# A graph attention and mixture-of-experts kernel: tiles in fill order, first weights loaded per tile, both expert results of a token side by side

## The reference

```
x = x + gnn(layernorm(x), edges, ...)          # two attention layers, 4 heads and 1 head
xf = layernorm(x)
probs = softmax(xf @ gate_w + gate_b);  top2_vals, top2_idx = top_k(probs, 2)
for each expert e:  h = gelu(xf @ W1[e] + b1[e]);  y = h @ W2[e] + b2[e]
out += (weight of e for the token, else 0) * y
x = x + out
```

## Time and profile before

| | us |
|---|---|
| median of 3 runs | 6120.17 |
| lowest, highest | 6066.71, 6154.52 |
| the profiled execution, its own time | 6092.53 |
| its span | 6090.7 |

### The profile page before, as it was taken

The page is one execution under the profiler, slowest core; times in us unless marked ns, Lnnn a source line. Parts: engine busy times, 40 slices in busy tenths (PEclk is TensorE's granted clock), DMA queues, the critical chain, the costliest instruction groups (busy, mean ns, idle before and its releaser), DMA issues. The chain is left out here.

```text
span 6090.7 us, 75071 instructions
## 1 busy us (share of the span) xinstructions
PE 3576.1 (59%) x12549; PEld 2299.2 (38%) x12550; DVE 3420.2 (56%) x8873; ACT 1636.8 (27%) x3595; POOL 3368.1 (55%) x3575
## 2 busy tenths in 40 slices
PE   5455555565555555554556666566666656624994
PEld 3233333333333333332333333333333333312773
DVE  7555555555555555555555555555555555531444
ACT  3222222222222222221233332322233333311222
POOL 4655555555555555555555555555655555644222
PEclk8666667766777777776676666666666676667997
DMA  4344444444444444443444444444444444442224
GB/s 127 104 109 108 105 108 110 109 107 106 109 108 109 110 110 110 110 104 86 111 114 114 115 114 114 113 114 114 114 113 114 114 113 114 118 137 86 91 64 155
DMA packets 321285, 670.43 MB, mean 110 GB/s; under 512 B 76855, under 2 KB 152773, under 8 KB 320938
## 3 DMA queue, kind: packets, MB, share of 16 engines
q0 software_dynamic: 170848, 469.37, 29.3%
q1 hardware_dynamic: 148585, 199.90, 11.5%
q10 hardware_dynamic: 1792, 0.53, 0.0%
HBM read 602.38 MB, written 75.12 MB: 111 GB/s over the span
## 5 line engine op out<-in xcount | busy, mean ns | idle before, releaser
L1002 POOL DMA_INDIRECT rows<-table,idx x3200 | 3031.4, 947 | 2086.8 <-issue 925.9
L1149 PE MATMUL bank<-rows,hit 128*128 128x260 f32 (+1 forms) x6464 | 2655.5, 553 | 2049.4 <-DVE acc L1257 1033.4
L1149 PEld LDWEIGHTS bank<-rows,hit 128*128 128x128 f32 x6464 | 1538.6, 265 | 2916.4 <-issue 1406.1
L1257 DVE TENSOR_TENSOR acc<-acc,bank 128x260 f32 (+1 forms) x3232 | 1356.4, 420 | 1385.5 <-remote 569.6
L1032 ACT ACTIVATE arg<-arg 128x32 f32<-128x32 f32 (+1 forms) x404 | 88.4, 219 | 3415.3 <-DVE arg L1237 2364.4
L1244 DVE TENSOR_TENSOR rows<-rows,bank 128x1024 f32<-128x1024 f32 x808 | 946.0, 1212 | 11.1 <-issue 9.7
L1211 DVE TENSOR_TENSOR hit<-bank,dst_loc 128x256 f32<-128x256 f32 x1616 | 671.7, 417 | 69.9 <-issue 58.6
L1222 DVE TENSOR_REDUCE bank<-bank 128x64 f32<-128x192 f32 (+1 forms) x404 | 115.4, 286 | 667.5 <-remote 598.8
L1026 ACT ACTIVATE hit_t<-gap,ones 128x1024 bf16<-128x1024 bf16 x404 | 463.8, 1148 | 20.3
L1021 ACT ACTIVATE gap<-loc,minus_node 128x1024 bf16<-128x1024 bf16 x404 | 462.6, 1145 | 11.7 <-DMA loc<-loc_row 11.5
L1138 PE MATMUL bank<-du,hit_t 128*128 x3232 | 340.9, 182 | 129.9 <-issue 127.6
(11 more groups left out here) (223 smaller groups left out, 2191.9 us busy)
## 6 DMA issues: line engine op xcount, KB each, us to landing
loc<-loc_row SPq DMA_DIRECT2D x404, 256.0 KB
rows<-table,idx POOLq DMA_INDIRECT x3200
sent<-zeros SPq DMA_DIRECT2D x202, 68.3 KB
xe<-sent SPq DMA_DIRECT2D x106, 128.5 KB
got<-back SPq DMA_DIRECT2D x96, 128.0 KB, 3.4
fw<-in_L_ffn_W SPq DMA_DIRECT2D x16, 512.0 KB, 9.0
table<-acc POOLq DMA_DIRECT2D x49, 130.0 KB
table<-acc SPq DMA_DIRECT2D x49, 128.5 KB
```

Source lines behind the costliest of these rows:

```text
L1002: pool.indirect_dma_start(rows[:, way, n, 0:R], None, table, bass.IndirectOffsetOnAxis(idx[:, way, n:n + 1], 0)).then_inc(rows_in[way], 16)
L1149: nc.tensor.matmul(sum_bank[n % 4][:, 0:R], hit[:, way, n, :], rows[:, way, n, 0:R], start=True, stop=True).then_inc(summed, 1)
L1257: nc.vector.tensor_tensor(kp.acc[:, t, 0:R], kp.acc[:, t, 0:R], sum_bank[n % 4][:, 0:R], ALU.add).then_inc(added, 1)
```

## The change

- **start_phase**: x is loaded in pairs of tiles, eight places for four. The attention vectors are loaded as rows (four transfers for twelve) and turned by TensorE. Ranking is laid along partitions (49 rows of 49), placing is done by TensorE with 14 short matmuls. The 1e-5 of the norm moves into ScalarE's square root. The windows are planned at other tiles (ITEMS_AT 9 for 6). Twelve constants more are made on GpSimd.
- **shift_phase**: ws lies in a PSUM bank and not in SBUF.
- **route_phase and expert_phase become one block.** W1 is no longer kept in SBUF: the W1 of a tile's expert (512 KB) is loaded for each of the 106 tiles into a ring of four (load_weights). A table gives the expert and the row of the k-th tile to be worked on: the tiles are ranked by the token tile up to which the sends must have come to fill them. GpSimd sends first and second copies of a token tile in turn, the home being changed in between for this tile alone, first 8 tiles, then one before every second store. A tile is loaded when the sends up to (k+7)//2 have landed.
- **expert tiles**: up is computed turned, as eight matmuls of 128 columns with W1 as the weights, so that turn_h, the copy of its result and VectorE's b1 go; ScalarE adds b1 within four Gelu activations of 128 columns that read PSUM. TensorE's order is turn_x(k+2), up(k+1), down(k).
- **combine_phase**: the rows 2t and 2t+1 of back hold the two results of token t, and one transfer of 256 KB loads both for 128 tokens.

The diff, cut to its core:

```
                 def rank_tiles():
 
                     dve.wait_ge(c_ready, 1)
-                    done.then_wait(nc.vector.tensor_copy(c[:, :], kp.bank[4][:, 0:NT + 1]))
-
-                    done.then_wait(ts(start[:, :], c[:, 0:NT], -1.0, 0.0, ALU.add, ALU.max))
-                    done.then_wait(tt(length[:, :], c[:, 1:NT + 1], start[:, :], ALU.subtract))
-                    done.then_wait(nc.vector.scalar_tensor_tensor(key[:, :], length[:, :], 8192.0, low[:, 0:NT],
+                    done.then_wait(ts(start[:, :], kp.bank[4][0:NT, 0:NT + 1], -1.0, 0.0, ALU.add, ALU.max))
+                    done.then_wait(tt(length[:, :], kp.bank[4][0:NT, 64:64 + NT + 1], start[:, :], ALU.subtract))
+                    done.then_wait(nc.vector.scalar_tensor_tensor(key[:, :], length[:, :], 8192.0, low_key[:, :],
                                                                   ALU.mult, ALU.add))
-                    done.then_wait(tt(less[:, :, :], key[:, :].unsqueeze(1).to_broadcast([P, NT, NT]),
-                                      key[:, :].unsqueeze(2).to_broadcast([P, NT, NT]), ALU.is_lt))
+                    done.then_wait(ts(less[:, 0, :], key[:, 0:NT], key[:, NT:NT + 1], None, ALU.is_lt))
+                    done.then_wait(tt(less[:, 1, :], less[:, 0, :], length[:, 0:NT], ALU.mult))
                     done.then_wait(nc.vector.tensor_reduce(rank[:, :], less[:, :, :], AX.X, ALU.add))
...
+                    done.then_wait(tt(end[:, :], rank[:, 1:2], length[:, NT:NT + 1], ALU.add))
+                    tt(place_of[:, 1:2], start[:, NT:NT + 1], rank[:, 1:2], ALU.subtract).then_inc(within_ready, 1)
+                    ts(by_rank[:, :], kp.col[0:NT, 0:NT], rank[:, 0:1], tile_id[:, :], ALU.is_equal, ALU.mult
+                       ).then_inc(within_ready, 1)
+                    done.then_wait(ts(past[:, :], item_row[:, :], end[:, :], None, ALU.is_ge))
+                    nc.vector.scalar_tensor_tensor(within[:, :], item_row[:, :], rank[:, 1:2], past[:, :],
+                                                   ALU.is_ge, ALU.subtract).then_inc(within_ready, 1)
...
+                    dve.wait_ge(items_placed, 1)
+                    placed = kp.bank[5][:, 0:2 * BLOCKS].rearrange("p (b c) -> p b c", c=2)
+                    nc.vector.tensor_copy(eb.order[:, :], kp.bank[5][0:1, 64:64 + NT])
+                    done.then_wait(nc.vector.tensor_single_scalar(low_of[:, :], placed[:, :, 0], float(NT * P), ALU.add))
+                    done.then_wait(tt(win_f[:, :], placed[:, :, 1], item[:, :], ALU.add))
...
+                    for m, a in enumerate((a_src, a_dst)):
+                        act.dma_start(vec[n][m * H:(m + 1) * H, :], a).then_inc(att_in[n], 16)
+                act.wait_ge(xt_zeroed, 2)
...
-        ws = b.sb(f"ws_{layer}", [P, NT, HEADS], F32)
+        ws = kp.bank[2][:, 0:NT * HEADS].rearrange("p (t h) -> p t h", t=NT)
...
+                def load_weights(k, way):
+                    e = sp.value_load(fb.table_of[0:1, bass.ds(k, 1)], min_val=0, max_val=X - 1)
+                    if not number(k) or k >= RING:
+                        sp.wait_ge(gelu_ready, (k - RING + 1) * HC)
+                    sp.dma_start(w1[:, way % RING, :, :], fw1[bass.ds(e, 1)].rearrange("o (c p) n -> p (o c) n", p=P)
+                                 ).then_inc(w1_in[way % RING], 16)
+
+                def load(k, way, turn):
+                    if not number(k) or k + 2 < T:
+                        load_weights(k + 2, way + 2)
+                    j, after = way % 2, (way + 7) // 2
+                    row = sp.value_load(fb.table_of[0:1, bass.ds(k + T, 1)], min_val=0, max_val=(T - 1) * P)
+                    if not early(k):
+                        sp.wait_ge(x_turned, k - 1)
+                        sp.wait_ge(home_ready, k - 1)
+                    if not number(k) or turn * 4 + after < NT:
+                        sp.wait_ge(second_sent[after % 4], (turn + after // 4 + 1) * 16)
+                    sp.dma_start(xe[:, j, :], kp.sent[bass.ds(row, P), :]).then_inc(x_in[j], 16)
...
+                sp.wait_ge(table_ready, 1)
+                load_weights(0, 0)
+                load_weights(1, 1)
+                for t in range(3):
+                    sp.wait_ge(second_sent[t], 16)
+                turns = (NT - 4) // 4
+                for k in range(8):
+                    load_both(k, k, 0)
+                with sp.Fori(1, turns) as turn:
...
+                def send_second(t):
+                    few = LAST if t == NT - 1 else P
+                    pool.wait_ge(first_sent[t % SENDS], 16 * (t // SENDS + 1))
+                    nc.gpsimd.iota(kp.acc[:, t, D:D + 1], [[0, 1]], base=(SLOT_TILES + 2 * t) * P + 1, channel_multiplier=2,
+                                   allow_small_or_imprecise_dtypes=True).then_inc(home_moved, 1)
+                    pool.wait_ge(home_moved, t + 1)
+                    if t >= 4:
+                        pool.wait_ge(second_sent[t % 4], 16 * (t // 4))
+                    pool.indirect_dma_start(kp.sent, bass.IndirectOffsetOnAxis(fb.slot[0:few, 1, t:t + 1], 0),
+                                            kp.acc[0:few, t, 0:D + 1], None).then_inc(second_sent[t % 4], 16)
+
+                def send(t):
+                    if t < NT:
+                        send_second(t)
+                    if t + SENDS < NT:
+                        send_first(t + SENDS)
...
+                for t in range(SENDS):
+                    send_first(t)
+                for t in range(FIRST):
+                    send(t)
+                for k in range(T):
+                    if k % 2 == 0:
+                        send(k // 2 + FIRST)
+                    store(k)
...
+                def up(k, way, turn):
+                    j = way % 2
+                    pe.wait_ge(w1_in[way], (turn + 1) * 16)
+                    pe.wait_ge(xet_ready, k + 1)
+                    if not early(k):
+                        pe.wait_ge(gelu_ready, (k - 1) * HC)
+                    for h in range(HC):
+                        for c in range(2):
+                            last = nc.tensor.matmul(kp.bank[2 + j][:, h * P:(h + 1) * P],
+                                                    w1[:, way, c, h * P:(h + 1) * P], xet[:, j, c * P:(c + 1) * P],
+                                                    start=(c == 0), stop=(c == 1))
+                    last.then_inc(up_done, 1)
...
+                def step(k, way, turn):
+                    j = way % 2
+                    if not number(k) or k + 2 < T:
+                        turn_x(k + 2, j, turn * 2 + way // 2 + 1)
+                    if not number(k) or k + 1 < T:
+                        up(k + 1, (way + 1) % RING, turn + (way + 1) // RING)
+                    down(k, way, turn)
...
-                def gelu(k, j):
-                    act.wait_ge(hid_ready, k + 1)
-                    nc.scalar.activation(hid[:, j, :], hid[:, j, :], ACT.Gelu).then_inc(gelu_ready, 1)
-
+                def gelu(k, way):
+                    j = way % 2
+                    act.wait_ge(up_done, k + 1)
+                    act.wait_ge(bias_ready, k + 1)
+                    if not early(k):
+                        act.wait_ge(down_done, k - 1)
+                    for h in range(HC):
+                        nc.scalar.activation(hidt[:, j, h * P:(h + 1) * P], kp.bank[2 + j][:, h * P:(h + 1) * P],
+                                             ACT.Gelu, bias=b1_now[:, way, h:h + 1]).then_inc(gelu_ready, 1)
...
-                    for a in range(2):
-                        sp.dma_start(got[0:few(t), j, a, :], kp.back[bass.ds((t + a * NT + SLOT_TILES) * P, few(t)), :]).then_inc(got_in[j], 16)
+                    sp.dma_start(got[0:few(t), j, :, :],
+                                 kp.back[bass.ds((2 * t + SLOT_TILES) * P, 2 * few(t)), :].rearrange(
+                                     "(p a) d -> p a d", a=2)).then_inc(got_in[j], 16)
```

More of the change, by code:

```diff
@@ L349, in _ @@
                              ).then_inc(windows_written, 16)
+                for t in range(SETS, XSETS):
+                    load(t)
                 sp.wait_ge(pads_ready, 2)
@@ L375, in _ @@
                 sp.wait_ge(tile_written, 32)
-                sp.wait_ge(loc_written, 16 * BLOCKS)
+                for j in range(2):
+                    sp.wait_ge(loc_written[j], 16 * ((BLOCKS + 1 - j) // 2))
             @block.vector
@@ new lines, in down @@
+                def down(k, way, turn):
+                    j = way % 2
+                    e = expert(k)
+                    if not early(k):
+                        pe.wait_ge(y_ready, k - 1)
+                    for h in range(HC):
+                        pe.wait_ge(gelu_ready, k * HC + h + 1)
+                        last = nc.tensor.matmul(kp.bank[6 + j][:, 0:D], hidt[:, j, h * P:(h + 1) * P],
+                                                fb.w2[:, e, h, :], start=(h == 0), stop=(h == HC - 1))
+                    last.then_inc(down_done, 1)
```

(8 more changed lines are left out.)

640 lines of the change are left out of this document (329 added, 311 removed).

## The result

The changed kernel took 6472.7 us (median of 4) where the kernel before took 6113.9: a ratio of 1.060, 95% interval 1.052 to 1.069. I had forecast 6330, with a range up to 6480. The direction and the loop came as forecast; the expert stage's term was too small by 158 us, the combination gained 10 us more than forecast, and a term that I had put at nothing, the shift buffer in PSUM, was worth 24 us.

What follows compares the result with a forecast made beforehand. It took a loop through SP's in-order queue to bound the changed expert stage: W1's load waits for Gelu, xe's follows. Start -33, routing -127.5, experts +394, combination -6 gave +228 us: 6320, set at 6330, range 6140 to 6480.

Steps and rivals of the forecast that it cites:

- the loop: Expert tiles: xe's load waits behind W1's, which waits for an earlier tile's Gelu; 7.95 us a tile, stage +394 us.
- the shift buffer: Shift phase: moving one buffer to PSUM costs nothing, since VectorE's pass over 12,544 elements goes element by element either way.
- 104 P + 8 - 607: Whole kernel: change in us, with P the expert tile's period; zero at P = 5.76, +122 us at 6.95.
- turn_x begins to up ends: Expert tile's period: 2.1 us at full clock, 4.1 at half, a quarter of the periods at the lower.
- from W1's issue to xe landed: Expert tile's period, DMA on SP's queue: 3.9 us taken, bounds 3.3 and 4.35.
- The likeliest case: Expert tiles: period 7.95 us, stage +394 us, total 6330; chance 0.61 for periods from 6.95 to 9.5.
- the third rival: Expert tiles: half clock all through or W1 queued behind scatters, P = 9.5, +389 us, 6480; chance 0.15.
- The first rival: Expert tiles: xe not held up by W1, clock full, P = 6.5, total +77 us, 6170 to 6200; chance 0.17.
- The second rival: Expert tiles: loads run ahead enough, 410 us for 440.5, total -197 us, 5900 to 5930; chance 0.07.
- Routing: Routing to first expert tile: tile 0 needs only ten sends, its load landing at 5439 for 5566.6, -127.5 us.
- Start phase: Before the edge phases: shorter ranking, placing, column loads and waits on VectorE; -33 us, bounds -20 and -45.
- Combination: After the expert tiles: 49 loads of 256 KB for 98 of 128 KB, engines still full; -6 us, bounds 0 and -14.

## Why the prediction was off in size

**The loop was right, the sum of its period was not.** The forecast was 104 P + 8 - 607 over the profiled 6092.5. With the measured P of 9.46 it gives 6092.5 + 385 = 6477 us; the profiled execution took 6475.8. That it meets so closely is in part luck, since what the rest had wrong cancels: shift phases -24.1 for 0, edge phases +26.1 for 0, combination -15.7 for -6, start and routing -155.4 for -160.5. The failed step is the sum of the period, 7.95 us where 9.46 was measured. Its terms, as forecast and as measured:
- *turn_x begins to up ends*: "a quarter of the periods at the lower" clock, 2.6 us. Measured 3.61, between 2.2 and 4.1 in single tiles; read between those two levels, three quarters. This was +1.0. The step took its share of the lower clock from means over stretches of other stages (0.77 and 1.00), and not for the part of the tile that stands in the loop behind the wait. Four matmuls in the wait brought the term down to 2.30.
- *from W1's issue to xe landed*: 3.9, bounds 3.3 and 4.35. Measured 1.29 + 3.21 = 4.50, +0.6, above my upper bound. That bound took the 1.3 us between the issues as running wholly beside the weights' transfer and then gave xe its share of bytes alone; the runs have xe at 2.0 us after its own issue with nothing ahead, and at 3.1 behind 512 KB.
- *Gelus and SyncE's wake*: 1.25 + 0.2, measured 1.36, -0.1.

**The likeliest case and the third rival.** "P = 9.5: +389 us, 6480", at a chance of 0.15, has the number that came, but only in part its reasons. It was not "half clock all through": the stage's mean is 0.80. "W1 queued behind scatters" is not seen either: W1 landed after 3.7 us, sooner than the 4.0 assumed. What came is the lower clock in most of turn and up, and xe slow behind W1. The case deserved more than 0.15, since both terms could lie near their dear ends at once.

**The first rival** (xe not held up, clock full, P = 6.5) is what the kernel without reloads and the one with xe ahead of the weights behind the same wait come to (6.84 and 6.48, ratios 1.018 and 1.011 on the second kind of chip), not the changed kernel.

**The second rival** (loads run ahead enough, 410 us for 440.5, ratio 0.97) was wrong of this kernel and right of what it would be without the loop: with leads of two tiles the stage takes 411 to 420 us and the kernel 0.967.

**Routing.** Forecast -127.5, measured -125.1. I had the first turn at 5439, 45 us behind the start of the block at 5394; it came 47.4 behind it. What was gained is the sends' time, as the run with all sends first shows.

**Start phase.** Forecast -33, measured -30.3 at the shift phase's first instruction.

**The shift buffer.** "One shift buffer moved to PSUM costs nothing" was right for VectorE, whose pass takes 13.21 us either way, and missed what ran beside it: GpSimd's gather lost the whole of that pass before and loses nothing after. Measured -24.1 for 0. In the first comparison the edge phases' +26.1 hides it; in the run of the start phase and this buffer on the second kind of chip it is most of the 27 us that the start phase leaves over.

**Combination.** Forecast -6, bounds 0 and -14; measured -10.5 for the reads (-10.6 undone), inside, but -15.7 for all from the last scatter to the end, outside. I had argued that the engines stay as full. Over the whole stage they were 0.79 busy at 265 GB/s and are 0.81 busy at 311: with the same share of their time they carry a sixth more. A further 5.2 us went between the last scatter and the first read (11.6 before, 6.4 after). They are no part of the pairs, as undoing those leaves 6.4; they come back (11.8) in the kernel that sends everything before its first store. Why, no run shows.

## What to carry to other kernels

When a load that needs little is issued on one in-order queue behind a load that waits for the consumer's own output, draw the loop: its period is the sum of every latency in it, and saving instructions or arithmetic outside it does not shorten it. Give both the same lead, in buffers, before anything else is tuned: here it was worth 594 of 6,504 us, against at most 305 (of 5,338, on the second kind of chip) for taking the loop's own costs down one by one. Where an engine waits once per period, price its first work behind the wait at the lower clock (here 3.61 us against 2.17 at the full one), not at the stage's mean. And a buffer's place matters to the engine beside: ask who runs during a long pass, not only who makes it.

## What the chip showed that I had not expected

- TensorE's clock was still granted in full during most of an idle wait of 4 us, fell about when the work began (between 1.7 us before and 1.4 us after), and was back in the eight matmuls of down (the three stretches above). Doing 3.6 us more work per tile in the wait made the kernel 125 us faster.
- A transfer of 128.5 KB lands 2.0 us after its issue with no weights ahead, 2.3 behind 256 KB and 3.1 behind 512 KB issued 1.3 us before it.
- GpSimd's gather took 13.8 us beside a VectorE pass of 13.2 us with both operands in SBUF, and 0.95 us beside the same pass with one operand in PSUM.
- Two kinds of chip: the kernel before takes 6,115 us on one and 4,977 on the other, and the changed kernel's routing block begins 1,138 us earlier (5365.8 and 4227.6) with the expert stage alike (992.6 and 988.7). In the edge phases single operations cost the same; TensorE's idle time before the line of the large matmuls is what differs, as these rows of the changed kernel show, on the first kind and on the second:

```profile
L1077 POOL DMA_INDIRECT rows<-table,idx x3200 | 3023.4, 945 | 2121.8 <-issue 917.0 <-PE bank L1224 733.1 <-ACT idx L1089 299.4
L1224 PE MATMUL bank<-rows,hit 128*128 128x260 f32 (+1 forms) x6464 | 2595.2, 540 | 2124.5 <-issue 1204.5 <-DVE acc L1332 831.2 <-DVE rows L1319 80.0
```

```profile
L1077 POOL DMA_INDIRECT rows<-table,idx x3200 | 3025.9, 946 | 987.3 <-issue 926.0 <-PE bank L1224 50.3 <-ACT idx L1089 11.0
L1224 PE MATMUL bank<-rows,hit 128*128 128x260 f32 (+1 forms) x6464 | 2627.9, 546 | 902.0 <-DVE acc L1332 890.2 <-DVE rows L1319 1.2
```

GpSimd's gathers take 945 ns in both, but it stands idle for 2,122 us before them in the one and for 987 in the other. The cause isn't known from these runs. So the same loss in the expert stage shows as a larger ratio on the second kind (1.073 against 1.065).
